# ScalarE takes ffn0's norms and the key-value evictions of a six-block kernel, with three small edits beside it

## The reference

```python
x = x + 0.5 * ffn0(norm(x))
x = x + attn0(norm(x))
x = x + 0.5 * ffn0(norm(x))      # the same weights again
x = x + 0.5 * ffn1(norm(x))      # "mid"
x = x + attn1(norm(x))
x = x + 0.5 * ffn1(norm(x))      # "last", the same weights again

norm(x) = (x - mean(x)) / sqrt(var(x) + 1e-5)           # over the 128 features
ffn0(h): scores = softmax(h @ gate_w.T); the best 2 of 8 by scores + gate_b
         y_e = swiglu((h @ w1[e].T + b1[e]) * (h @ w3[e].T + b3[e])) @ w2[e].T + b2[e]
         the two y_e weighted by their scores, plus a shared expert of the same form
attn0(h): q, k, v = h @ Wqkv.T + b;  32 heads of 4;  ctx = (q k^T) v without softmax
          ctx normed over tokens and head features, * gn_w + gn_b, @ out_w.T + out_b
ffn1(h): the best 1 of 8 by h @ Wg.T;  gelu(norm(h) @ W1[e] + b1[e]) @ W2[e] + b2[e]
attn1(h): 8 heads of 16 with rotary positions and gates, a linear recurrence over the tokens
```

## Time and profile before

| what | value |
|---|---|
| three runs | 1300.01, 1302.91, 1305.37 us; median 1302.91 |
| profiled execution | 1299.59 us, its span 1297.8 us |
| busy, share of the span | PE 1093.7 us (84%), DVE 1081.1 (83%), ACT 814.5 (63%), POOL 661.9 (51%) |
| chain that ended last | DVE 37%, PE 31%, ACT 14%, POOL 7%, issue 6%, SP's queue 3%, DMA 2% |
| mean granted TensorE clock | 0.949 of full speed |

### The profile page before, as it was taken

One profiled execution on the slowest core, in us unless ns is written; L12 is line 12 of the kernel. 1 busy time (PEld: TensorE's weight loads), 2 busy tenths in 40 slices (PEclk: granted clock), 3 DMA queues, 4 the chain that ended last, 5 costly groups with the idle time before them and its releaser, 6 DMA issues.

```text
span 1297.8 us, 37970 instructions
## 1 busy us (share of the span) xinstructions
PE 1093.7 (84%) x14412; PEld 874.6 (67%) x14412; DVE 1081.1 (83%) x3558; ACT 814.5 (63%) x1354; POOL 661.9 (51%) x727
## 2 busy tenths in 40 slices
PE   2865888798889878878886799989889999899997
PEld 1543766677767667756776687877767777677775
DVE  6689999989898989998988879785897898877663
ACT  2454768547656646546574767786856775667562
POOL 1067766677777777777777525232143354310010
PEclk9977999999999999999998979989989998999789
DMA  9101443534355343223434312221110010100000
GB/s 298 35 32 57 111 123 91 121 88 114 99 119 132 80 100 92 77 78 87 115 97 115 81 41 63 64 61 44 39 28 25 22 49 18 34 3 18 3 18 26
DMA packets 172950, 94.01 MB, mean 72 GB/s; under 512 B 98540, under 2 KB 163207, under 8 KB 172647
## 3 DMA queue, kind: packets, MB, share of 16 engines
q1 hardware_dynamic: 115958, 35.84, 11.8%
q0 software_dynamic: 16384, 33.59, 9.6%
q10 hardware_dynamic: 40432, 22.17, 6.2%
HBM read 25.98 MB, written 45.61 MB: 55 GB/s over the span
## 4 chain that ended last, share of the span: by engine, by line
DVE 37%; PE 31%; ACT 14%; POOL 7%; issue 6%; SPq 3%; DMA 2%; ACTq 0%; POOLq 0%; DVEq 0%
PE bank L750 5%; POOL rows L1873 4%; DVE heads_store L1084 3%; DVE x L1116 3%; SPq L1937 3%; PE bank L811 2%; PE sums L978 2%; PE bank L961 2%; DVE stats_head L1073 2%; PE bank L797 2%; PE bank L766 2%; PE bank L575 1%; DVE heads_store L1162 1%; PE bank L830 1%; DVE store L1603 1%
## 5 line engine op out<-in xcount | busy, mean ns | idle before, releaser
L1873 POOL DMA_INDIRECT rows<-store,r_slot x256 | 260.1, 1016 | 136.0 <-issue 73.2
L1889 POOL DMA_INDIRECT y_in<-ys,r_result x256 | 263.2, 1028 | 79.2 <-issue 70.5
L750 PE MATMUL bank<-u_xp,w_hi 128*128 128x128 f16 x2432 | 224.5, 223 | 14.1 <-DMA u_xp<-rows 4.9
L750 PE MATMUL bank<-u_xp,w_lo 128*128 128x128 f16 x1216 | 216.7, 223 | 0.0
L750 PEld LDWEIGHTS bank<-u_xp,w_hi 128*128 x2432 | 192.3, 100 | 23.3 <-issue 18.6
L750 PEld LDWEIGHTS bank<-u_xp,w_lo 128*128 x1216 | 121.3, 100 | 0.1
L1842 POOL TENSOR_SCALAR ve_last<-mv_last 128x4 f32<-128x4 f32 x16 | 3.2, 197 | 172.9 <-DVE mv_last L1077 172.6
L575 PE MATMUL bank<-heads_store,w_hi 128*128 128x512 f16 x256 | 81.4, 401 | 8.7 <-DVE heads_store L1162 1.9
L1116 DVE SCALAR_TENSOR_TENSOR x<-y_in,r_weight,x 128x128 f32<-128x128 f32 x256 | 72.9, 347 | 1.1
L1842 POOL TENSOR_SCALAR ve_front<-mv_front 128x4 f32<-128x4 f32 x16 | 3.1, 197 | 133.7 <-DVE mv_front L1077 133.4
L811 PE MATMUL bank<-w_packed,heads_store 128*128 128x128 f32 x512 | 66.8, 285 | 0.0
(11 more groups left out here) (409 smaller groups left out, 3259.5 us busy)
## 6 DMA issues: line engine op xcount, KB each, us to landing
ys<-u_y_even ACTq DMA_DIRECT2D x38, 256.0 KB
ys<-u_y_odd ACTq DMA_DIRECT2D x38, 256.0 KB
u_xp<-rows SPq DMA_TRANSPOSE x304
x<-x_dram SPq DMA_DIRECT2D x16, 256.0 KB, 5.6
rows<-store,r_slot POOLq DMA_INDIRECT x256
y_in<-ys,r_result POOLq DMA_INDIRECT x256
out_dram<-x SPq DMA_DIRECT2D x16, 256.0 KB, 2.7
rows<-blank SPq DMA_DIRECT2D x48, 64.0 KB
```

What stands on the lines that cost most here:

```text
L750: ins = pe.matmul(B[:, of_block[j]], of_expert(wp, e, F16, part, which), xp_rows[:, xp, of_block[j]], start=(n == 0 and j == 0), stop=(n = ...
L1873: pool.indirect_dma_start(row_dram[g], bass.IndirectOffsetOnAxis(route.slot[g][:, i, t:t + 1].bitcast(U32), 0), rows[:, groups[g].first * ...
L1889: pool.indirect_dma_start(fetch.y[i][:, t, k, :], None, y_dram[g], bass.IndirectOffsetOnAxis(route.result[g][:, k, t0 + t:t0 + t + 1].bitc ...
```

## The change

- ffn0's norm: VectorE's step 1 computes only minus mean times root for the four tiles (`away`); ScalarE's step 1 begins with four activations, one a tile, with that as bias and the root as scale, waits for them, and goes on to the high part as before.
- Key-value evictions: they move to ScalarE, directly behind its query eviction, as plain copies. The bias is added in PSUM by one more matmul for each of the two passes; VectorE splits the bias into three bfloat16 parts once, in the preparation (`split_rows`, also used for the other row biases).
- The factor one half leaves the routing weights and stands in the unit evictions on ScalarE.
- ffn1's logits are read in PSUM by `first_best`; the bank comes free two operations later.
- The middle ffn1 lanes get an own store for the normed rows and their transposes and don't wait for the heads any more; the last lanes move to the places that the middle ones had. The strings in `turns` are the same.

```diff
+        kv_bias = sb("kv_bias", [P, 2 * D], BF16)
+            s.away = sb("away_" + s.name, [P, T])
...
+        mid_store = sb("mid_store", [P, 4, N])
         for i, s in enumerate(mids + lasts):
-            norm_buffers(s, piece(heads_store, 2 * i, 1, T), piece(heads_store, 2 * i + 1))
+            source = mid_store if s in mids else heads_store
+            norm_buffers(s, piece(source, 2 * (i % 2), 1, T), piece(source, 2 * (i % 2) + 1))
...
                         B = bank(s.name, "kv", c, b)
+                        on.wait_ge(*prep.by_vector.at("kv_bias"))
+                        pe.matmul(B[:], ones_b[:], kv_bias[:].unsqueeze(1).broadcast_to([P, BATCH_TILES, 2 * D]),
+                                  start=True, stop=False, skip_group_check=True)
...
-                        ring.free_at((s.name, "kv", c, b), s.by_vector, "kv", c, b)
+                        ring.free_at((s.name, "kv", c, b), s.by_scalar, "kv", c, b)
...
-                    ring.free_at((s.name, "logits1", c), s.by_vector, "lg1", c)
+                    ring.free_at((s.name, "logits1", c), s.by_vector, "mask", c, "ge")
...
                 elif j == 1:
-                    normed(s, c, ("ffn0", l), s.xn0)
+                    on.wait_ge(*s.by_pool.at("rstd", ("ffn0", l), c))
+                    mark(dve.scalar_tensor_tensor(s.away[:], s.mv[:, :, 0], -1.0, s.rstd[:], ALU.mult, ALU.mult),
+                         "away", l, c)
...
                     split_experts()
+                    split_rows(const["a0_bkv"][0:3, :], kv_bias[0:3, :], "kv_bias")
...
-                elif k == 3:
-                    bias = const["a0_bkv"][:].unsqueeze(1).broadcast_to([P, BATCH_TILES, 2 * D])
-                    for b in range(NB):
-                        on.wait_ge(*s.by_tensor.at("kv", c, b))
-                        mark(dve.tensor_tensor(
-                            s.kv[:, b * BATCH_TILES:(b + 1) * BATCH_TILES, :],
-                            ring[s.name, "kv", c, b][:].rearrange("p (j n) -> p j n", j=BATCH_TILES), bias,
-                            ALU.add), "kv", c, b)
...
-                    mark(dve.tensor_reduce(s.share[:], s.of[:], AX.X, ALU.add), "share_of", l, r)
-                    on.wait_ge(*at("share_of", l, r))
-                    mark(dve.tensor_scalar(s.weight[g][:, :, here], s.share[:], 0.5, None, ALU.mult),
-                         "weight", l, r)
+                    mark(dve.tensor_reduce(s.weight[g][:, :, here], s.of[:], AX.X, ALU.add), "weight", l, r)
...
-                    if c < 2:
+                    if c < 2 and s in lasts:
                         after_heads(on)
...
-                    mark(dve.tensor_copy(s.lg[:], ring[s.name, "logits1", c][:, 0:T * E]
-                                         .rearrange("p (t e) -> p t e", e=E)), "lg1", c)
-                    on.wait_ge(*at("lg1", c))
...
-                    first_best(s, s.lg[:], s.m1, s.ge, s.i1, s.mask[:, :, 0:3, 0:E], T, "mask", c)
+                    lg = ring[s.name, "logits1", c][:, 0:T * E].rearrange("p (t e) -> p t e", e=E)
+                    first_best(s, lg, s.m1, s.ge, s.i1, s.mask[:, :, 0:3, 0:E], T, "mask", c)
...
-                    on.wait_ge(*s.by_vector.at("xn", ("ffn0", l), c))
+                    on.wait_ge(*s.by_vector.at("away", l, c))
+                    for t in range(T):
+                        ins = act.activation(s.xn0[:, t, :], xc(c)[:, t, :], ACT.Identity, bias=s.away[:, t:t + 1],
+                                             scale=s.rstd[:, t:t + 1])
+                    mark(ins, "xn0", l, c)
+                    on.wait_ge(*s.by_scalar.at("xn0", l, c))
...
                     mark(act.activation(s.qt, ring[s.name, "q", c][:], ACT.Identity, bias=const["a0_bq"][:]),
                          "q", c)
+                    for b in range(NB):
+                        on.wait_ge(*s.by_tensor.at("kv", c, b))
+                        mark(act.copy(s.kv[:, b * BATCH_TILES:(b + 1) * BATCH_TILES, :],
+                                      ring[s.name, "kv", c, b][:].rearrange("p (j n) -> p j n", j=BATCH_TILES)),
+                             "kv", c, b)
...
-                    mark(act.copy(s.y[:], ring["units", "y", l, g, u][:]), "y", *use)
+                    mark(act.activation(s.y[:], ring["units", "y", l, g, u][:], ACT.Copy, scale=0.5), "y", *use)
```

More of the change, by code:

```diff
@@ L295, in build @@
         route.moved = sb("r_moved", [P, 2, most * T])
-        route.share = sb("r_share", [P, 2, batch])
         route.shift = sb("r_shift", [P, E])
@@ L320, in build @@
         mids, lasts = ([lane(f"{name}{i}") for i in range(2)] for name in ("mid", "last"))
+        mid_store = sb("mid_store", [P, 4, N])
         for i, s in enumerate(mids + lasts):
-            norm_buffers(s, piece(heads_store, 2 * i, 1, T), piece(heads_store, 2 * i + 1))
+            source = mid_store if s in mids else heads_store
+            norm_buffers(s, piece(source, 2 * (i % 2), 1, T), piece(source, 2 * (i % 2) + 1))
             s.xp = s.xt.bitcast(F16).rearrange("p (k n) -> p k n", k=2)
-            s.gs = [piece(heads_store, 2 * i), piece(heads_store, 2 * i + 1)]
-            s.lg, s.ge = (heads_store[:, 14 + j, 384 + T * E * i:384 + T * E * (i + 1)]
-                          .rearrange("p (t e) -> p t e", e=E) for j in range(2))
+            s.gs = [piece(source, 2 * (i % 2)), piece(source, 2 * (i % 2) + 1)]
+            s.ge = heads_store[:, 15, 384 + T * E * i:384 + T * E * (i + 1)].rearrange("p (t e) -> p t e", e=E)
             s.m1 = sb("m1_" + s.name, [P, T])
@@ L588, in attn0 @@
                         B = bank(s.name, "kv", c, b)
+                        on.wait_ge(*prep.by_vector.at("kv_bias"))
+                        pe.matmul(B[:], ones_b[:], kv_bias[:].unsqueeze(1).broadcast_to([P, BATCH_TILES, 2 * D]),
+                                  start=True, stop=False, skip_group_check=True)
                         for j in range(BATCH_TILES):
                             t = b * BATCH_TILES + j
[L591 to L592 removed]
+                            ins = pe.matmul(B[:, j * 2 * D:(j + 1) * 2 * D], s.xt[:, by_t[t]], const["a0_wkv"][:],
+                                            start=False, stop=(j == BATCH_TILES - 1), skip_group_check=True)
                         s.by_tensor.mark(ins, "kv", c, b)
[L594 removed]
+                        ring.free_at((s.name, "kv", c, b), s.by_scalar, "kv", c, b)
                 elif k == 4:
@@ L1236, in split_biases, with split_rows @@
                 on.wait_ge(*at("bias_f"))
-                rest, row = bias_f, row_bias[0:3].rearrange("p e d -> p (e d)")
+                split_rows(bias_f, row_bias[0:3].rearrange("p e d -> p (e d)"), "row_bias")
+            def split_rows(rest, row, done):
+                mark, at, n = prep.by_vector.mark, prep.by_vector.at, row.shape[1]
+                part, left, total = bias_part[:, 0:n], bias_rest[:, 0:n], bias_sum[:, 0:n]
                 for k in range(3):
-                    mark(dve.tensor_copy(bias_part, rest), "bias_part", k)
-                    on.wait_ge(*at("bias_part", k))
+                    mark(dve.tensor_copy(part, rest), done, "part", k)
+                    on.wait_ge(*at(done, "part", k))
                     if k < 2:
-                        dve.tensor_tensor(bias_rest, rest, bias_part, ALU.subtract)
+                        dve.tensor_tensor(left, rest, part, ALU.subtract)
                     if k == 0:
-                        mark(dve.tensor_scalar(bias_sum, bias_part, ident[0:3, 0:1], None, ALU.mult), "bias_sum", k)
+                        mark(dve.tensor_scalar(total, part, ident[0:3, 0:1], None, ALU.mult), done, "sum", k)
                     elif k == 1:
-                        mark(dve.scalar_tensor_tensor(bias_sum, bias_part, ident[0:3, k:k + 1], bias_sum, ALU.mult,
-                                                      ALU.add), "bias_sum", k)
-                    else:
-                        mark(dve.scalar_tensor_tensor(row, bias_part, ident[0:3, k:k + 1], bias_sum, ALU.mult,
-                                                      ALU.add), "row_bias")
+                        mark(dve.scalar_tensor_tensor(total, part, ident[0:3, k:k + 1], total, ALU.mult,
+                                                      ALU.add), done, "sum", k)
+                    else:
+                        mark(dve.scalar_tensor_tensor(row, part, ident[0:3, k:k + 1], total, ALU.mult,
+                                                      ALU.add), done)
                     if k < 2:
-                        on.wait_ge(*at("bias_sum", k))
-                    rest = bias_rest
+                        on.wait_ge(*at(done, "sum", k))
+                    rest = left
             def split_experts():
@@ L2026, in _ @@
             eng.memset(row_bias[:], 0.0)
+            eng.memset(kv_bias[:], 0.0)
             eng.memset(const["sel1"][:], 0.0)
```

2 lines of the change are left out of this document (1 added, 1 removed).

## The result

The changed kernel takes 1332.24 us (median of 4 runs, 1329.79 to 1335.91), the kernel before 1304.14 beside it (4 runs): ratio 1.0218, 95% interval 1.0176 to 1.0259. It is slower by 28 us, where 1293 was forecast. Its profiled span is 1330.4 us, against 1297.8. The granted TensorE clock doesn't explain this: the four runs have 0.934 to 0.938, and in eight later runs of the kernel before at 0.933 to 0.938 it took 1301 to 1309 us.

A forecast was written before the change was run, and what follows sets the result against it. From 72 to 707 us VectorE was fullest (89%) but GpSimd, occupied 592.6 of 635 us, limited gains; afterwards TensorE bound. There -24, +7 and +7 made -10; with +1.8 before and -2 after, -10: 1293 us, range 1277 to 1311.

The forecast's parts named there:

- rival (b): ffn0 step: ScalarE becomes the late engine, 27 us for 17 chunks, net +12, so 1315 us; chance 0.17.
- Busy times: From 72 to 707 us: VectorE falls from 566 to 516 us, ScalarE rises from 388 to 453, GpSimd stays occupied 593.
- Start: Before 72 us: bias splitting adds 2.9 us, three moved norms give back 1.1; net +1.8, first scatter about 74 us.
- Small edits: Halved weights, logits copy and middle norms' buffer: about -2 us on the end, after 707 us.
- The waits for ScalarE: ffn0 step: about half of 29 VectorE rests stand up to 1.3 us, a third on the chain; some +7 us.
- The -24 on the chain: From 72 to 707 us: 25.9 us of removed VectorE work on the chain, replaced by products of about 2; at most -24.
- GpSimd halves what is won: From 72 to 707 us: GpSimd's 31.9 us of slack must shrink, so it takes half of the remaining gain; +7 us.
- The evictions: Key-value evictions in 16 chunks: 19 us off VectorE, 19 more on ScalarE, with the chain shorter at the chunk read.
- 15 us of the chain's gain: From 72 to 707 us: gain that the slower rival let the chain keep, subtracted from its added waits to give +12.
- (a): Cover on both sides: GpSimd's and TensorE's orders absorb all but a few microseconds; 1301 us, chance 0.33.
- (c): The full amount: the -24, +1.8 at the start and the logits' whole 5.9 us; 1275 us, chance 0.05.
- (d): The norms hold up GpSimd's scatters; moving them wins up to 33 us more, 1265 us; chance 0.02.

The follow-up runs named there:

- e18: The changed kernel with ffn0's norms back on VectorE, beside the kernel before on a chip like the first: 1310.04 us, ratio 1.0059.
- e4: The kernel before with only the small edits (half at the store, logits read in PSUM, middle norms' own store), on a slower chip: ratio 1.0023.
- e15: The kernel before with ffn0's norm left out and no ScalarE passes, high part and rest taken from x, on a slower chip: ratio 0.9951.

## Why the prediction was wrong

The forecast was 1293, within 1277 to 1311; measured were 1332. The outcome is on the side of rival (b), ScalarE becomes the late one, forecast at 1315 with a chance of 0.17, and beyond it.

- **Busy times: right.** VectorE 519 us against 516, ScalarE 452 against 453, GpSimd unchanged. Four passes 1.65 us against 1.6 (482 ns each); the product 156 ns against 187; the evictions 586 ns each on ScalarE.
- **Start: nearly right.** First scatter 72.16, forecast 74. With the norms back (e18) it is 74.78: the splitting costs 2.7 us (2.9 forecast), and what the norms gave back covered it all, not 1.1 of it.
- **Small edits: not decided.** The lag falls from 35 to 32.6 us over the last stretch, about -2.5 against -2; but in e18, with the same edits, it goes from 7.8 to 8.2, so the fall can't be put down to them. Alone, on another chip, e4 can't tell them from nothing.
- **The waits for ScalarE: mis-sized, and this is the step that failed.** "of 29 rests about half stand up to 1.3 us, and a third of them lie on the chain, some +7". Measured: 21 stand, 1.8 us in the mean and up to 3.9, 37.8 us together against 4.6, and 41 us of the passes lie on the chain. Its working had the rest ready 2.6 us after the product's start, 0.4 later than before, which holds only with ScalarE free when the product is done. In the step shown above ScalarE begins 0.84 us after the product's start, and the rest after 3.27. And it let VectorE's earlier arrival count as won, while it counted the later readiness for a third. It is the readiness that sets when the row is stored: 1.03 us in the mean against those 0.4, 30 us in 29 steps. e18 shows what the norms' way costs: with them back the rest's wait is 5.2 and 21 us return. That nearly all of it is the later rest is what the waits suggest, not what a run isolates. The sum had +7 for this term.
- **The -24 on the chain: wrong in kind.** Removed work on the chain shortens it only if its replacement is shorter. 1.15 us of VectorE became 1.65 us of ScalarE with a product ahead, in the same place of the same chain. e15, which had neither norm nor passes, won 0.5% on its chip.
- **GpSimd halves what is won: wrong in sign.** Its 31.9 us of slack were taken for a ceiling of the gain, and nothing in the sum let them grow. They became 70.6, and the growth of 38.7 is as large as the lag of 35.
- **The evictions: wrong in sign.** "Here the chain gets shorter" was read at one chunk in which ScalarE was ready early. The prediction let ScalarE's next work go back by 1.2 us and put that at nothing: with the evictions there VectorE's waits ahead of the units grow from 11.4 to 23.2 us (e18). The bias matmuls, taken as covered, now lie on the chain in places. With the norms back the rest of the change costs 8 us (e18).
- **Rival (b) itself** had the place right and the price low: it charged 1.6 us in 17 chunks and set 15 us of the chain's gain against it. Without those 15 it would have read 1330, near the measured 1332, but partly by luck: it had nothing for the evictions, which with the small edits make 8 us, and 27 for norms that cost some 21. Its evidence against, 39% idle time of ScalarE, counted for little: the waits grew all the same.

(a), cover on both sides, is out by the 35 us. (c) and (d) too: GpSimd's scatters kept their time (mean 1017 ns for 1016) with ffn0's norms beside them gone, so there is no sign that these held them up. The 1265 of (d) doesn't follow from its 33 us either (1302.9 - 33 = 1270). The Trainium skill, "ScalarE: Activation LUTs", section "Rules for kernel authors", advises VectorE for additions and multiplications; the outcome agrees: 482 ns a tile against 359, 1.65 us against 1.25 for the same four tiles.

## What to carry to other kernels

With fixed orders on several engines, price a moved operation by the length of the dependent step it stands in and by what stands behind it in the new engine's list, not by either engine's idle share: work that leaves a chain is won only if what replaces it is shorter. Slack of an engine downstream is no ceiling on the effect of a change; it grows as readily as it shrinks. Read at every chunk, not at one, how long before the consumer the value was ready, and take the new length off that.

## What the runs showed of the hardware

- A 128x128 ScalarE pass with two per-partition operands takes 482 ns (477 to 497 over 116), 1.65 us for four.
- The first of them came with a table load (ACT_TABLE_LOAD) of 1.28 us, at the start and beside a longer wait. It isn't added by the change; before, the first high part had it:

```profile
L1651 ACT ACT_TABLE_LOAD x1 | 1.3, 1283 | 12.9 <-DVE away_head L1136 12.9
```

```profile
L1653 ACT ACT_TABLE_LOAD x1 | 1.3, 1283 | 14.6 <-DVE heads_store L1084 14.6
```

- The same kernel took 1332 us on one chip and 1655 on another: TensorE at a granted clock of 0.849 for 0.938, the same matmul (line 755) at 236 ns for 224 in the mean, and much more "issue" time ahead of weight loads, with the other engines' busy times within 1%. Three chips were like the second. What sets them apart no run tells.
